# New stage orders and a new layout of PSUM banks in the windowed transformer stack

## The reference

```
q, k, v = split(shift(x) @ Wqkv)              # 16 heads of 64
q, k = rotary(l2norm(q) * qs), rotary(l2norm(k) * ks)
x = local_attention(q, k, v) @ Wo + x         # windows of 32 queries, 64 keys, causal
xn = layernorm(shift(x)) * g + b
a, gate = split(xn @ W1 + b1)
x = (a * gelu(gate)) @ W2 + b2 + x
```

## Time and profile before

| what | value |
|---|---|
| time, median of 3 runs | 3840.44 us (3836.24 to 3842.03) |
| profiled execution, its own time | 3854.52 us |
| its span, first to last instruction | 3852.7 us |
| mean granted clock of TensorE | 0.976 |
| TensorE busy | 3558.6 us (92%) |
| VectorE busy | 3244.9 us (84%) |
| ScalarE busy | 2526.3 us (66%) |
| GpSimd busy | 1548.6 us (40%) |

### The profile page before, as it was taken

How to read it: one execution, slowest core, us unless ns; L and a number is a source line. 1 busy time by engine, 2 the same in 40 slices (tenths; PEclk the granted TensorE clock), 3 DMA queues, 4 the chain that set the end, 5 groups by cost and what they waited for, 6 DMA issues and landing times. The chain is left out here.

```text
span 3852.7 us, 123346 instructions
## 1 busy us (share of the span) xinstructions
PE 3558.6 (92%) x51360; PEld 2002.7 (52%) x51360; DVE 3244.9 (84%) x3701; ACT 2526.3 (66%) x3406; POOL 1548.6 (40%) x924
## 2 busy tenths in 40 slices
PE   5999769989999999999999999999999999999996
PEld 2333235555555555555555555555555555555553
DVE  7999678878888888888888888888888888888884
ACT  4888646656757666666666757667666666666663
POOL 2333234334434444434444344343443444344440
PEclk7999879999999999999999999999999999999998
DMA  1000121111121111121111111111111111211112
GB/s 29 2 1 1 32 69 27 34 28 32 34 55 34 28 37 30 27 62 28 38 28 27 40 52 36 28 27 39 55 34 28 32 34 27 62 28 38 28 27 61
DMA packets 60817, 130.63 MB, mean 34 GB/s; under 512 B 15988, under 2 KB 31864, under 8 KB 60408
## 3 DMA queue, kind: packets, MB, share of 16 engines
q1 hardware_dynamic: 60408, 124.06, 13.4%
HBM read 23.58 MB, written 4.19 MB: 7 GB/s over the span
## 5 line engine op out<-in xcount | busy, mean ns | idle before, releaser
L1027 PE MATMUL slot<-w_qkv,xs 128*128 (+1 forms) x2304 | 1106.7, 610 | 46.0 <-ACT xs L880 28.2
L746 POOL TENSOR_TENSOR half_sq<-sq 128x1024 f32<-128x1024 f32 x192 | 501.1, 2610 | 1509.4 <-ACT sq L888 1489.6
L751 POOL TENSOR_TENSOR cosq<-cosq,sinq 128x1024 f32<-128x1024 f32 x384 | 902.2, 2366 | 371.4 <-DVE sinq L798 371.4
L888 ACT ACTIVATE sq<-slot 128x1024 f32<-128x1024 f32 x384 | 392.2, 1021 | 413.0 <-PE slot L1027 412.9
L1027 PEld LDWEIGHTS slot<-w_qkv,xs 128*128 128x128 f32 x2304 | 412.0, 193 | 454.3 <-issue 445.3
L796 DVE TENSOR_TENSOR cosq<-slot,table 128x1024 f32<-128x1024 f32 x384 | 467.8, 1218 | 146.1 <-ACT sq L888 135.5
L824 DVE TENSOR_TENSOR qk<-cosq,ry 128x1024 f32<-128x1024 f32 x384 | 518.0, 1359 | 13.7 <-ACT ry L945 11.4
L798 DVE TENSOR_TENSOR sinq<-slot,table 128x1024 f32<-128x1024 f32 x384 | 465.7, 1213 | 0.0
L978 PEld LDWEIGHTS slot<-ident,qk 128*128 128x128 f32 x3072 | 350.4, 141 | 215.7 <-issue 125.4
L978 PE MATMUL slot<-ident,qk 128*128 128x128 f32 x3072 | 396.9, 275 | 37.1 <-DVE qk L824 32.9
L996 PE MATMUL slot<-kT,qT 64*32 64x64 f32 x24576 | 296.2, 225 | 53.1 <-issue 53.1
(11 more groups left out here) (123 smaller groups left out, 4950.6 us busy)
## 6 DMA issues: line engine op xcount, KB each, us to landing
vb<-va SPq DMA_DIRECT2D x720, 130.0 KB, 2.3
w_qkv<-in_w_qkv SPq DMA_DIRECT2D x21, 512.0 KB, 5.5
w_o<-in_w_o SPq DMA_DIRECT2D x6, 512.0 KB
w<-in_w SPq DMA_DIRECT2D x6, 342.0 KB
res<-in_x SPq DMA_DIRECT2D x4, 512.0 KB, 6.1
kept<-res SPq DMA_DIRECT2D x1, 2048.0 KB, 8.7
out<-fin_res SPq DMA_DIRECT2D x8, 256.0 KB, 2.4
w<-in_w SPq DMA_DIRECT2D x6, 171.0 KB
```

The source lines that it names most:

```text
L746: nc.gpsimd.tensor_tensor(half_sq[:, :, :], squares[:, :, 0, :], squares[:, :, 1, :], ALU.add).then_inc(S["folded"], 1)
L751: nc.gpsimd.tensor_tensor(cosq[:, side], cosq[:, side], sinq[:, side], ALU.add).then_inc(S["qk"[side] + "_added"], 1)
L888: nc.scalar.activation(sq[:, "qk".index(name)].rearrange("p h d -> p (h d)"), flat(name, n), ACT.Square).then_inc(S[name + "_squared"], 1)
L1027: last = nc.tensor.matmul(slot(kind, n)[:, i, :], xs[:, n * P:(n + 1) * P], w_qkv[:, (0 if layer is None else layer) % 2, "qkv".index(kind ...
```

## The change

The change rewrites the five lists of stages (SyncE's stays as it is) and the slots. No stage is added or removed, and no instruction of a stage is altered.

```diff
 PE_ORDER = stages(
-    "q0 k0 qT3- kT3- r2- s3- vb2- k1 va2- kT0 q1 qT0 v0 r3- k2 va3- vb3- s0 q2 wo- qT1 r0 v1 kT1 centre- vb0 va0 "
-    "var- q3 v2 s1 k3 qT2 h0- kT2 h1- r1 h2- s2 vb1 v3 va1 y- ")
+    "k0 q0 qT3- kT3- r2- s3- vb2- k1 va2- r3- q1 vb3- va3- v0 kT0 q2 qT0 k2 s0 wo- qT1 kT1 r0 v1 centre- vb0 s1 "
+    "var- q3 qT2 va0 k3 r1 h0- kT2 h1- s2 h2- va1 v2 vb1 v3 y- ")
 DVE_ORDER = stages(
-    "rotate_q0 rotate_k0 norms0 s3- scale_k0 vb2- scale_q0 va2- rotate_k1 turn2- rotate_q1 va3- vb3- turn3- "
-    "norms1 s0 scale_q1 rotate_q2 residual- scale_k1 rotate_k2 norms2 vb0 va0 scale_k2 scale_q2 z- rotate_q3 s1 "
-    "rotate_k3 turn0 hid0- norms3 hid1- hid2- s2 scale_q3 vb1 va1 scale_k3 turn1 y- ")
+    "rotate_k0 rotate_q0 norms0 s3- vb2- scale_k0 va2- rotate_k1 turn2- va3- vb3- scale_q0 turn3- rotate_q1 "
+    "norms1 s0 scale_q1 scale_k1 rotate_q2 residual- rotate_k2 norms2 vb0 scale_q2 s1 z- rotate_q3 scale_k2 va0 "
+    "rotate_k3 norms3 hid0- hid1- s2 hid2- turn0 vb1 va1 scale_k3 scale_q3 y- turn1 ")
 ACT_ORDER = stages(
-    "v3- square_q0 square_k0 qT3- kT3- r2- norm0 square_k1 kT0 exp3- qT0 square_q1 r3- v0 square_q2 norm1 "
-    "square_k2 exp0 shift- qT1 r0 kT1 square- norm2 v1 root- square_q3 v2 affine- square_k3 qT2 exp1 to_gelu- "
-    "gate0- kT2 gate1- r1 gate2- to_exp- norm3 next exp2 ")
+    "next- v3- square_k0 exp2- square_q0 qT3- kT3- r2- norm0 exp3- square_k1 r3- square_q1 v0 kT0 qT0 square_k2 "
+    "norm1 square_q2 exp0 qT1 shift- r0 kT1 norm2 square- v1 root- square_q3 exp1 qT2 affine- square_k3 r1 "
+    "to_gelu- kT2 gate0- gate1- gate2- to_exp- v2 norm3 ")
 POOL_ORDER = stages(
-    "fold1- add_q1- add_k1- add_q2- fold2- add_k2- fold3- add_q3- add_k3- fold0 add_k0 add_q0 ")
+    "fold2- add_q2- add_k2- fold3- add_q3- add_k3- fold0 add_k0 add_q0 fold1 add_q1 add_k1 ")
...
 SLOTS_OF = (
-    "q0 r2 vb2 q1 vb3 q2 r0 centre k3 r1 va1",
-    "kT3 s3 kT0 qT0 r3 va3 s0 qT1 kT1 va0 v2 qT2 kT2 s2 y",
-    "k0 va2 v0 wo v1 s1 h1 vb1",
-    "qT3 k1 k2 vb0 q3 h0 h2 v3",)
+    "qT3 r2 vb2 r3 vb3 q2 kT1 s1 va0 h1 v2 y",
+    "q0 k1 v0 qT0 s0 qT1 v1 qT2 r1 kT2 s2 vb1",
+    "kT3 va2 va3 kT0 k2 centre k3 h2 v3",
+    "k0 s3 q1 wo r0 vb0 q3 h0 va1",)
```

## The result

The changed kernel takes 3896.11 us (median of 4 runs, 3891.81 to 3905.00) against 3841.24 us before: ratio 1.0147, 95% interval 1.0127 to 1.0168, so 1.5% slower. On another chip it measured 1.0147 again (1.0130 to 1.0165). The profiled span went from 3852.7 to 3903.2 us.

What follows compares the result with a forecast made beforehand. TensorE, busy 92% of the span, was taken as the bound, so order can win only its waits. 9 - 37 + 16 + 56 = +44 us gave 3884 us beside the median; 8-in-10 range 3822 to 3912 us.

Steps and rivals of the forecast that it cites:

- Start of the step: On ScalarE, exp2' between the squares of q0 and k0 makes s3' start 0.2 later, at 7.14: +9 us.
- Waits that go: TensorE's waits at kT0 (20.4 us), s0 (7.7) and kT1 for qT1's copy (9) vanish: -37 us.
- Switches: On TensorE, some four more edges between projections and small-tile products, 0.35 us a step (bounds 0 and 0.6): +16 us.
- The middle of the step: From s3' to kT1: GpSimd's fold2 blocks VectorE's scale_q1, rotate_q2 ends late, kT1 waits 1.2 us a step: +56 us.
- v2 and next later: At the step's end, y' stands 4.7 behind v2, about 0.7 to spare; next's copies lie under y': no cost.
- The relief by issue gaps: TensorE's issue gaps between va3' and s0 shorten the wait at kT1, from 1.3 to 1.2 us a step.
- The faster rival: scale_q1 and scale_k1 run before fold2, so kT1's wait is gone: 3828 us, with free switches 3812; chance 0.18.

Runs made afterwards that it cites:

- Experiment 2: Changed kernel with exp2' moved on ScalarE ahead of v3', right behind next: 3885.07 us, ratio 1.0096 to the kernel before.
- experiment 3: Changed kernel with v2 moved on TensorE ahead of va1, beside h2: 3848.76 us, ratio 1.0000 to the kernel before (12 runs, 3824.22 to 3879.29).
- experiment 1: Changed kernel with add_q2 ahead of fold2 in GpSimd's order: 3875.40 us, ratio 1.0072 to the kernel before.
- experiment 5: Changed kernel in which GpSimd folds the squares of tile 2 twice, first into a spare buffer: 4088.49 us, ratio 1.0627 to the kernel before.
- experiment 6: Changed kernel with a small 128x128 add into a spare buffer on GpSimd ahead of fold2: 3919.79 us, ratio 1.0192 to the kernel before.
- experiment 7: Changed kernel with 64 short instructions ahead of TensorE's loop, shifting its body in memory: 3885.59 us, ratio 1.0113 to the kernel before.
- experiment 10: The kernel of experiment 1 with TensorE's loop shifted by 64 instructions as well: 3838.36 us, ratio 0.9978 to the kernel before (13 runs, 3831.76 to 3861.90).
- experiment 4: Changed kernel with three edits together (add_q2 ahead of fold2, exp2' ahead of v3', v2 beside h2): 3794.77 us, ratio 0.9869 to the kernel before.

## Why the prediction was right, step by step

It said 3884 us, 44 us slower than before, with one mechanism for most of it. Measured: 3896 and 55 us.

- **Start of the step**, s3' at 7.14: 7.17 in the timeline. Experiment 2 shows that the cause was right and the term (9 us) small by 3: the copy of qT3' moves with the square, and r2' waits for it.
- **Waits that go**, 37 us: both rows have gone (20.4 and 7.7 us). Missing was the wait that replaces them in part: k2 now stands in kT0's slot, and ScalarE copies kT0 only after v0 (until 2055.08 in the step above). From qT0 to k2 it is 1.07 instead of 0.87: 0.2 a step, 9 us that no term held. The weight loads of that stage show the wait in all 45 steps (12.4 us, the PEld row above). It is the largest part of the 11 us by which the sum was short. No run tests it.
- **Switches**, 16 us: experiment 3 measured one projection taken from between products at 0.32 a step, within the bounds of 0 and 0.6 for all four. The choice inside the bounds is not tested by itself.
- **The middle of the step.** s0 at 24.9: it starts at 26.69 in a step with a gap of issue of 1.36 at vb2', so 25.3 without. The walk said that VectorE works without a hole until 24.1; it had three (0.30, 0.81, 0.31) and ended at 25.7. GpSimd's adds and the scores both came 1.6 to 1.7 later than walked, and so the order of fold and scale was kept, since both chains hang on the same stages, as the prediction says. The fold ahead of the scale by 0.5: 0.51. kT1's wait 1.2: 1.17 on average. r0 without a wait: none. Experiments 1, 5 and 6 show the cause by taking it away, doubling it and turning its order round.
- **v2 and next later**, nothing: y' has no wait in the rows.
- **The relief by issue gaps** is the one step whose picture was too simple. I took 0.1 a step off the wait for gaps between va3' and s0. In the change no gap lay there, and that the wait came out at 1.17 all the same is luck; after the shift a gap did lie before wo', and it covered the wait (experiment 7). And gaps behind the wait count as well: without it, they took back half in one layout (1); in another (10) they took back 12 us in the profiled run, while the median shows no such loss. Why a place gets its gap only in some layouts stays open, and so does the spread of experiments 3 and 10.

The faster rival (the fold not in the way) is what experiment 1 built. The version that beats both is number 4, at 0.9869: it keeps the new order and mends the three places that the prediction priced.

## What to carry to other kernels

When an order of stages is judged, walk the chain of each engine to the one stage that waits, and look for instructions of VectorE and GpSimd that exclude each other on it: such a pair costs what is left of the first when the second wants to start (1.7 of 2.35 us here, of which 1.17 reached TensorE), and to turn the pair round wins nothing while the first still stands between the second and what follows it. Measure the small edits one by one and then together, as in experiment 4, and repeat a gain with the code shifted: up to 36 us here belonged to the layout of TensorE's code and not to the edit.

## What the runs showed of the hardware

- Where TensorE's instructions come late depends on where the loop lies in memory: a shift by 64 instructions moved gaps of 1 to 2 us to other stages and the time by 13 us and 36 us in two versions, and by nothing in a third. Each of these contains the 10 us that the shift adds once, where TensorE enters the loop (17.59 against 7.70 in experiment 7).
- Beside weight loads at 217 to 248 GB/s such a gap was 4.66 us and with small loads 1.91; the granted clock was 0.71 and 0.81 in the two windows of 7 us that hold the long gap and what follows it, and 1.00 with the short one.
- Standing still for 3.29 us was followed by about 3 us at the lower clock level (0.50, 1.2 GHz) in experiment 5; 0.88 us in the changed kernel was not (1.00). A wait that is three times as long thus cost more than three times as much (185 us on top of 55).
